# Causal attention in joint steps of two row tiles, with the mask added by TensorE, in a GNN and mixture-of-experts attention block

## The reference

```python
x = x + gnn(layernorm(x), edges)
idx_s, idx_t = argmax of the router's two halves
spatial_out  = spatial_experts(ln_s(x), idx_s)       # attention without a mask
xt = ln_t(x)
logits = einsum('bthd,bshd->bhts', q, k) * HD ** (-0.5)
causal = tril(ones((T, T), dtype=bool))
logits = where(causal, logits, -inf)                 # the causal attention
att = softmax(logits, axis=-1)
temporal_out = xt + (att @ v) @ pw.T + pb
fused = cross_mha(spatial_out, temporal_out)         # attention without a mask
x = x + fused
x = x + mlp(ln_mlp(x))
```

## Time and profile before

| | |
|---|---|
| median of 3 runs | 1917.43 us (1909.32 to 1918.24) |
| the profiled execution | 1921.58 us, its span 1919.8 us |
| PE busy | 1686.8 us (88%), 9816 matmuls |
| PEld busy | 1392.3 us (73%) |
| DVE busy | 1155.1 us (60%), 1886 instructions |
| ACT busy | 896.0 us (47%), 1736 instructions |
| POOL busy | 694.4 us (36%), 448 instructions |
| granted TensorE clock, mean | 0.947 |

### The profile page before, as it was taken

How to read it: one execution, slowest core, us unless ns; L and a number is a source line. 1 busy time by engine, 2 the same in 40 slices (tenths; PEclk the granted TensorE clock), 3 DMA queues, 4 the chain that set the end, 5 groups by cost and what they waited for, 6 DMA issues and landing times.

```text
span 1919.8 us, 27000 instructions
## 1 busy us (share of the span) xinstructions
PE 1686.8 (88%) x9816; PEld 1392.3 (73%) x9816; DVE 1155.1 (60%) x1886; ACT 896.0 (47%) x1736; POOL 694.4 (36%) x448
## 2 busy tenths in 40 slices
PE   2898999579999999789978788799999997799998
PEld 1566776358788888677767677577888886578776
DVE  7994226430798898521167777415888887763333
ACT  3893312221687878321156665214888775311000
POOL 3022010044354452132454643226365358243330
PEclk9998999779999999798989999799999998899999
DMA  3000000233111210042212123011211220011111
GB/s 100 7 23 23 0 28 27 75 109 70 28 28 28 55 39 12 17 143 90 59 28 54 28 65 124 22 48 29 53 30 28 50 81 23 1 45 44 38 33 59
DMA packets 33000, 88.40 MB, mean 46 GB/s; under 512 B 5190, under 2 KB 5660, under 8 KB 32369
## 3 DMA queue, kind: packets, MB, share of 16 engines
q1 hardware_dynamic: 32881, 86.83, 16.8%
HBM read 43.29 MB, written 12.80 MB: 29 GB/s over the span
## 4 chain that ended last, share of the span: by engine, by line
PE 73%; DVE 15%; ACT 5%; issue 3%; DMA 1%; SPq 1%; POOL 1%; DVEq 0%; ACTq 0%; POOLq 0%
PE ps L575 11%; PE ps L778 11%; PE ps L576 11%; PE ps L577 11%; PE ps L758 10%; PE ps L747 8%; PE ps L748 6%; DVE ngm L1423 3%; DVE R L1432 2%; PE ps L696 2%; PE ps L800 2%; DVE R L1211 1%; PE ps L697 1%; DVE stats L1168 1%; ACT R L958 1%
## 5 line engine op out<-in xcount | busy, mean ns | idle before, releaser
L958 ACT ACTIVATE R<-ps 125x500 fp32r<-125x500 f32 (+3 forms) x624 | 295.3, 512 | 194.7 <-PE ps L758 194.1
L445 POOL TENSOR_TENSOR w_hi<-w_raw,zero 128x512 fp32r<-128x512 f32 x96 | 108.5, 1130 | 765.4 <-PE ps L577 475.2
L1423 DVE TENSOR_REDUCE ngm<-ps 125x1 f32<-125x1250 f32 (+5 forms) x240 | 303.2, 1264 | 65.0 <-PE ps L748 57.9
L1432 DVE TENSOR_TENSOR R<-ps,R 125x500 fp32r<-125x500 f32 (+3 forms) x624 | 326.8, 574 | 14.2 <-ACT R L958 14.0
L947 ACT ACTIVATE F<-ps,ngm 125x1250 f32<-125x1250 f32 (+5 forms) x240 | 276.3, 1151 | 71.2 <-DVE ngm L1423 68.2
L778 PE MATMUL ps<-R 125*128 125x252 f32 (+1 forms) x2080 | 301.7, 290 | 4.4 <-DVE F L1470 3.6
L747 PE MATMUL ps<-R 128*125 128x512 f32 (+4 forms) x624 | 247.3, 397 | 49.6 <-DVE R L1432 45.6
L758 PE MATMUL ps<-ident,F 125*125 125x125 f32 x2040 | 271.8, 278 | 10.1 <-ACT F L947 10.1
L778 PEld LDWEIGHTS ps<-R 125*128 125x128 f32 x2080 | 262.3, 191 | 6.5 <-DVE R L1432 5.4
L758 PEld LDWEIGHTS ps<-ident,F 125*125 125x125 f32 x2040 | 250.5, 193 | 14.4 <-ACT F L947 12.5
L575 PE MATMUL ps<-R,w_hi 128*128 128x512 f32 (+1 forms) x576 | 214.1, 372 | 42.0 <-POOL w_lo L460 14.1
(11 more groups left out here) (174 smaller groups left out, 2436.1 us busy)
## 6 DMA issues: line engine op xcount, KB each, us to landing
R<-F SPq DMA_DIRECT2D x96, 312.5 KB, 5.3
w_raw<-in_weights SPq DMA_DIRECT2D x96, 256.0 KB, 2.6
TB<-in_x SPq DMA_DIRECT2D x10, 250.0 KB
x_d<-F SPq DMA_DIRECT2D x10, 250.0 KB
zt_d<-F SPq DMA_DIRECT2D x1, 2500.0 KB, 8.7
F<-zt_d SPq DMA_DIRECT2D x1, 2500.0 KB, 13.6
qc_d<-F SPq DMA_DIRECT2D x4, 625.0 KB, 3.8
xt_d<-F SPq DMA_DIRECT2D x4, 625.0 KB, 3.4
```

The costliest lines, as they stand in the source:

```text
L445: return eng.tensor_tensor(to, a, zero[0:to.shape[0], :].to_broadcast(list(to.shape)), ALU.add)
L958: eng.activation(PT[0][:, g % 2, c0:c0 + nb, n % 2, 0:P], ps[0:P, 3 * (n % 2) + bank, 0:P * nb].rearrange("p (c t) -> p c t", c=nb), ACT.C ...
L1423: eng.tensor_reduce(out=ngm[0:P, n % 2:n % 2 + 1], in_=flat(n % 2)[0:P, 0:K.cols[i]], op=ALU.max, axis=AX.X, negate=True).then_inc(A.negma ...
L1432: eng.tensor_tensor(PT[1][blk], ps[0:P, 3 * (n % 2) + bank, 0:P * nb].rearrange("p (c t) -> p c t", c=nb), PT[0][blk].bitcast(F32), ALU.su ...
```

## The change

`Attn` gets a notion of parts. In the causal stage step k of a head (k = 0 to 4) handles tile 9 - k (10 - k blocks) and tile k (k + 1 blocks) together, always eleven blocks, 40 steps in place of 80. The scores of both stand in the same three banks, the small tile behind the large one. The mask is no more added by VectorE: TensorE adds it as one more product, of the unit matrix `ident_r` by `mask_r`, to the diagonal block. Maximum and exponential are two instructions in a step, with one semaphore. The eleven blocks are transposed three, four and four to a bank; copies and remainders go by runs that end at a bank or at a tile. Groups of values join two pairs of tiles (12 blocks, in two halves of six) or one (six blocks), three groups per head. At the first step of a head, half a group of values stands ahead of the transposes.

For all three stages: pads are no more cleared, and the semaphores are not incremented ahead, since waits of the first steps are left out; `comb` has two buffers; the keys' high part is cut in four pieces of up to 314 columns through a small `KT`; the reciprocals of the last pair, their copies and remainders are taken ahead of the last group's output; of the last three broadcasts the second uses bank 6 and waits only for the normalisation two before it. In the causal stage the widened inverses use `w_hi` and `w_lo` of one more unit, so only one unit of the next product is cut ahead.

The core of the diff:

```diff
+        big, small = NT - 1 - k, k
+        at = P * (big + 1)
+        at += at % 2
+        if at < 2 * BANK < at + P * (small + 1) and P * (small + 1) <= BANK:
+            at = 2 * BANK
+        return [(big, 0, big + 1, 0), (small, at, small + 1, big + 1)]
...
+        first, second = ((0, 4), (1, 3), (2, None))[m % 3]
...
-                        eng.tensor_tensor(KT[64:128, :], KS[b][64:128, :].bitcast(F32),
-                                          zero[64:128, :].to_broadcast([64, T]), ALU.add).then_inc(A.cut, 1)
+                        for part, sl in enumerate(K_CUTS):
+                            keys, top_ = KS[b][64:128, sl], KT[64:128, 0:sl.stop - sl.start]
+                            eng.tensor_tensor(top_, keys.bitcast(F32), zero[64:128, :].to_broadcast(list(top_.shape)),
+                                              ALU.add).then_inc(A.cut, 1)
+                            eng.wait_ge(A.cut, n0 + 2 + 2 * part)
+                            eng.tensor_tensor(keys, keys.bitcast(F32), top_.bitcast(F32), ALU.subtract
+                                              ).then_inc(A.cut, 1)
...
-                cut_units(u, u + 2)
+                cut_units(u, u + ahead(K))
...
+                        eng.matmul(piece, QSH[b][:, P * i:P * i + P], keys, start=True, stop=False)
+                        ins = eng.matmul(piece, QSL[b][:, P * i:P * i + P], keys, start=False, stop=not diagonal)
+                        if diagonal:
+                            d = max(at, d0)
+                            col = d - d0 + 1 - odd
+                            ins = eng.matmul(flat(n % 2)[0:P, d:to], ident_r[:, 0:P], mask_r[:, col:col + to - d],
+                                             start=False, stop=True)
...
+                for n in range(K.N + 2):
+                    h, k = divmod(n, K.S)
+                    if n + 1 < K.N:
+                        scores(K, n + 1)
+                    if K.causal and h and k == 0:
+                        values(K, 3 * h - 2, 6, 12)
+                    if n < K.N:
+                        turn_probs(K, n)
+                    if not K.causal:
+                        if n >= 2:
+                            values(K, n // 2 - 1, 5 * (n % 2), 5 * (n % 2) + 5)
+                    elif h and k == 1:
+                        values(K, 3 * h - 1, 0, 6)
+                    elif k in (2, 3) and n < K.N:
+                        values(K, 3 * h, 6 * (k - 2), 6 * (k - 2) + 6)
+                    elif k == 4:
+                        values(K, 3 * h + 1, 0, 6)
...
+                for j in range(3):
+                    if j:
+                        eng.wait_ge(A.norm, 3 * (K.pairs0 + H // 2 - 1) + j - 1)
+                    spread_inverses(K, H // 2 - 1, j, 7 - j % 2)
...
-                    if K.causal:
-                        block_ = flat(n % 2)[0:P, P * i:P * i + P]
-                        c(eng.tensor_tensor(block_, block_, mask, ALU.add))
...
+                    if n == K.N or K.per < n < K.N and n % K.per == 1:
+                        inverses(n // K.per - 1)
...
+                    if n == K.ends:
+                        inverses_lo(H // 2 - 1)
...
-            clear_pads()
```

More of the change, by code:

```diff
@@ L105, in __init__ @@
-        self.banks0 = (H // 2 + 1) * (0, full, full + half)[turn]
-        self.cuts0 = 7 * H * turn
+        self.S = NT // 2 if causal else NT
+        self.N = H * self.S
+        self.per = 2 * self.S
+        self.ends = self.N + (1 if causal else 0)
+        self.G = 3 if causal else HG
+        self.W = 12 * 252 if causal else NT * 252
+        self.spans = ((0, 3), (3, 4), (7, 4)) if causal else ((0, 2), (2, 4), (6, 4))
+        self.runs = [self.runs_of(k) for k in range(self.S)]
+        self.cum = [sum(len(r) for r in self.runs[:k]) for k in range(self.S + 1)]
@@ new lines, in runs_of, with super, bank, run @@
+    def runs_of(self, k):
+        found = []
+        for bank, (j0, count) in enumerate(self.spans):
+            for part, (_, _, blocks, first) in enumerate(self.parts(k)):
+                lo, hi = max(j0, first), min(j0 + count, first + blocks)
+                if lo < hi:
+                    found.append((bank, part, lo, hi))
+        return found
+    def super(self, n):
+        return self.supers0 + n + 1
+    def bank(self, n, b):
+        return 3 * (self.supers0 + n) + b + 1
+    def run(self, n, bank):
+        upto = sum(1 for r in self.runs[n % self.S] if r[0] <= bank)
+        return self.runs0 + n // self.S * self.cum[-1] + self.cum[n % self.S] + upto
@@ new lines, in chunks, with gathered @@
+    def chunks(self, m):
+        found = []
+        for at, (pair, offset, count) in enumerate(self.pairs_of(m)):
+            for c in range(count):
+                s = 1 if self.causal and c == count - 1 else 0
+                found.append((c, offset + 252 * c + 126 * s, 252 * at + 126 * s, 252 - 126 * s, c == 0, c == count - 1))
+        return found
+    def gathered(self, n):
+        if not self.causal:
+            return (n - 3) // 2 if n >= 3 and n % 2 else None
+        h, k = divmod(n, self.S)
+        if k == 3:
+            return 3 * h
+        return 3 * (h - 1) + 1 + k if h and k < 2 else None
@@ new lines, in broadcast @@
+    def broadcast(self, n):
+        if not self.causal:
+            q, k = n // self.per - 1, n % self.per
+            return (q, k // 4 - 2, (n - 5) // 2) if q >= 0 and k in (11, 15, 19) and n < self.N else None
+        for j, (k, head, g) in enumerate(((18, 2, 2), (20, 3, 0), (23, 3, 2))):
+            q = (n - k) // self.per
+            if n % self.per == k % self.per and 0 <= q < H // 2 - 1 and n <= self.N:
+                return q, j, 3 * (2 * q + head) + g
+        return (2, 2, 3 * 7 + 1) if n == self.N + 1 else None
@@ L1485, in attend @@
[L1485 to L1496 removed]
+                greatest(0)
@@ new lines, in attend @@
+                for n in range(K.N + 3):
+                    if n + 1 < K.N:
+                        greatest(n + 1)
+                    if n < K.N:
+                        probs_lo(n)
+                    if n and K.gathered(n - 1) is not None:
+                        output(K.gathered(n - 1))
+                    if n == K.N or K.per < n < K.N and n % K.per == 1:
+                        inverses(n // K.per - 1)
+                    if K.broadcast(n) is not None:
+                        pair, j, m = K.broadcast(n)
+                        normalise(pair, j, pair_bank(m))
+                    if n == K.ends:
+                        inverses_lo(H // 2 - 1)
```

476 lines of the change are left out of this document (237 added, 239 removed).

## The result

The changed kernel takes 1835.11 us (median of 4 runs, 1833.84 to 1836.76) beside 1915.83 us for the kernel before in the same comparison (1909.32 to 1918.24). The ratio is 0.9581, 95% interval 0.9563 to 0.9598: 80.7 us less. The prediction was 1827 us, with 1811 to 1853 as its range; 90 us less had been summed, and about 9 of them are missing.

The account below looks back on a forecast made before the run. No engine is full in the causal attention: a chain of handovers, closed by VectorE's loop, bounds it. Gains 73 (causal stage) + 15.5 (ends) + 2 (starts) - 0.5 (loads) = 90 us; 1917.4 - 90 = 1827, range 1811 to 1853.

Parts of the forecast that it names:

- The loop: Causal attention, joint step: maxima 1.57, remainders 1.76, last score bank 0.82, together 4.15 us, VectorE's loop last, TensorE close behind.
- the tail: Causal attention: 1.7 us added to 39 joint steps to reach the last exponential.
- a head's first step: Causal attention: value products ahead of the transposes delay copies and remainders, about +0.35 us once in five steps.
- steps with a broadcast: Causal attention: no separate term; 0.13 us a step (3%) added for what the first attention showed over its clean loop.
- The mask term: Causal attention: mask products on TensorE, in the last bank's part of the loop, cost 0.13 us a step.
- the 73: Causal attention: gain in us, from 244.2 to 171.4 between first maximum and last exponential.
- I cost it at nothing: GpSimd's longer key cuts in the causal stage: occupancy 39.7 of 43.5 us over two heads, so no time charged.
- the rival of late cuts: Causal stage: GpSimd's cuts late, two heads need some 46 us instead of 43.5; total 1836 us; chance 14%.
- The ends: Ends of the three attentions: earlier reciprocals and overlapped broadcasts save 6 us at two, 3.5 at the causal, together 15.5.
- the gain hoped for: First and third attention's ends: shortened gaps would keep the full clock, 1.3 us more than counted at each.
- Starts and loads: Stage starts: 2 us gained over three stages; causal end: residual loaded later, cost 0.5 us, bound 4.
- Rival 3: Stage ends bring nothing and the residual load is late: 1827 + 14 = 1841 us; chance 10%.

## Why the prediction was right, and where its steps were off

**The causal stage.** Predicted 171.4 us to the last exponential, measured 174.4. The loop was right in kind, its engines and its order; the mean period is 4.40 us (171.8 over 39) where 4.35 was summed, and the tail 2.6 where 1.7 was. A little luck is in the mean: the first two periods, with both sets of banks free at the start, take 7.26 us together, and the other 37 have a mean of 4.45. The clean steps are 4.09 to 4.41 beside 4.15. Two terms were small: a head's first step adds 0.6 us over the mean of the others, not 0.35, and steps with a broadcast add 0.4 to 0.8. The mask term was 0.13 and measured 0.13. Gain 69.5 for 73; the 73 was counted from the first mask addition, 0.3 us ahead of the first maximum. Some 10 of the 69.5 are the mask's move, by the run with the mask on VectorE. No run takes the joining of tiles back alone, so that the other 60 are its work rests on the steps' lengths as summed and measured.

**GpSimd.** "I cost it at nothing" held inside the stage. The occupancy while heads are cut was estimated at 39.7 of 43.5 and is 40 of 44; over the whole stage, with loads to wait for and nothing to cut at its end, GpSimd is busy for 73%. The measured time of 1835 happens to lie at the 1836 of the rival of late cuts, but its sign, scores that wait for GpSimd in this stage, isn't there. The rival had its price about right, 7.5 us for 46 us in two heads: eight pieces, with 44.8, cost 6.4. But the sentence was about the causal stage alone, and the same longer cuts run in the third attention, where ten residual rows and the next weights are queued behind them. **This is the step that failed**: of the third end it was asked what comes earlier, not who else must be ready by then. Of 6.5 us gained there 4.3 were given back, and the run with the rows split shows 3 to 3.5 of them. What was to be looked at was not only GpSimd's own work there but SP's queue: the last cut releases the loads for which GpSimd then waits 20 us.

The Trainium skill (GPSIMD Engine Reference, "Key points") says that GpSimd shares its SBUF interfaces with VectorE and slows beside instructions with two SBUF inputs. The prediction set it aside for the causal stage, rightly: its cuts take the same 2.27 us as in the earlier trace rows. At the end of the third attention the trace agrees with the rule: a weight cut takes 1.95 and 2.36 us beside VectorE's L1341 and 1.04 and 1.28 away from it. So late rows get later still. One row speaks against a simple rule: the instruction at 1532.58 keeps its 2.07 us although L1341 starts at 1533.36. No run here takes VectorE's instruction away, so the cause rests on their coincidence in time and on the page's rule; it is argued, not shown.

**The ends.** 6 + 6 + 3.5 were summed. Measured: 6.4 and 6.5 at the first and the third end by the table, 6.5 and 3.0 at the first and the causal end by undoing the edit. Against the kernel before, the causal end gained only 1.2, because the last joint steps leave more behind the last exponential than single tiles did (36 value products and twelve products of earlier broadcasts, where there were 28 and four): the edit's 3.0 less 1.8. That this tail grows was no term of the sum. The low clock was not the price feared, nor the gain hoped for: a gap of 1.24 us ahead of the first end's broadcasts left it at 1.00, one of 3.24 us ahead of the causal end's was followed by the fall 0.6 us later.

```profile
777.95 0.33 PE L918 MATMUL ps<-R,w_hi 125*128 125x126 f32 x1 [1.24 <-DVE F L1568]
...
1132.16 0.33 PE L918 MATMUL ps<-R,w_hi 125*128 125x126 f32 x1 [3.24 <-DVE F L1568]
...
1132.92 0.41 PE L918 MATMUL ps<-R,w_hi 125*128 125x126 f32 x1
```

**Starts and loads.** The rows settle both. TensorE's idle time ahead of the first scores fell from 1.26, 1.25 and 1.24 us to 0.30, 0.41 and 0.30 in the three stages, 2.7 us in all where 2 was summed. In the causal stage it shows in no row of the table, since the first tile now has ten blocks and not one, and its maximum starts 1.80 us behind the first scores where it started 0.85 behind (945.58 less 943.78, and 956.53 less 955.68):

```profile
943.78 0.47 PE L868 MATMUL ps<-R 128*125 128x512 f32 x1 [0.41 <-DVE F L1372]
```

The residual's load is issued at 1139.20 and lands 9.6 us later; its first use is at 1153.43, 16.8 us behind the last normalisation as before, and waits for a product. It cost nothing where 0.5 was summed. Rival 3 was priced at 14 us, less than the 15.5 of the ends that it takes away; by its own terms it stood at 1842 or more, and nothing else hangs on it.

**The sum.** Predicted 90, measured 80.7 by medians: 3.5 less in the causal stage, 2.3 less at its end, 4.3 given back at the third; less the 0.9 that the first and the third end brought over their 6 each, that is 9.2, against 9.3 missing. That the two agree so closely is partly luck: the starts and what executions differ by come to several us, either way.

## What to carry to other kernels

When a stage is shortened, list for each engine what is queued ahead of the first thing the next stage needs, and compare its end with the new time, in every stage that shares the code: a helper that was 3.5 us early became 4 us late here without having been touched. Moving work off the engine that closes a step's loop pays at most in those steps where that engine is last; the table of step periods tells which these are (0.46 us at one step, less than nothing at a head's first). Keeping the clock up in a gap is worth only what the products behind it don't wait for anyway.

## What the runs showed of the hardware

- The same idle gap of 2.30 us in the same code was followed by the lower clock in one execution (0.62 over four us) and by the full clock in another. At the start of the causal stage 1.80 us left it at 1.00, and 2.10 us in another kernel were followed by 0.57; 1.24 us ahead of the first end's broadcasts didn't bring it down. The Trainium skill (TensorE: Matmul & The Clock Gate, "HAM oscillation") says that idle gaps put the clock back; the traces agree for the gaps above 3 us (3.24 and 3.93 us, each with 0.50 behind it) and show both outcomes for the short ones.
- Idle products cover a gap at full clock (14 in 3.44 us), and come too late once the clock has fallen (5.29 us for the same 14).
- GpSimd: 64 rows by 314 columns in 0.71 us, 157 columns in 0.45, and 0.18 of idle time ahead of an instruction that waits for the one before it. Eight further instructions for the same columns lengthen a head's cuts by 2.4 us, 0.3 each.
- GpSimd's 2.07 us instruction took 5.86 us beside VectorE's subtraction of SBUF data, the largest such factor in these traces.
